# Late addition, accumulating transposes and predicated neighbour selection in a four-layer convolution kernel

## The chip, the cores and the metric

The kernel runs on one core of one Trainium2 chip. The metric is device time in microseconds (us). TensorE (PE), VectorE (DVE), ScalarE (ACT), GpSimd (POOL) and SyncE (SP) each run their own instruction stream and meet at semaphores. Everything is 32-bit float.

## The reference

x is 8 images of 64 channels, 96 x 96. Four layers in a row, each x + layer(groupnorm(x)):

```python
x = x + L0(gn(x))   # chunked linear attention (9 chunks of 1024 positions), group norm
x = x + L1(gn(x))   # offset conv, bilinear sampling at clipped offsets, 3x3 conv
x = x + L2(gn(x))   # 3x3 conv by FFT whose padded kernel makes it a sum over shifts
x = x + L3(gn(x))   # cosine similarities, offset-and-mask conv, deformable 3x3 conv
# L1, sampling at (cy, cx), both clipped to the image:
v_t = dy * (v_rt - v_lt) + v_lt
v_b = dy * (v_rb - v_lb) + v_lb
out = dx * (v_b - v_t) + v_t
# L3: four corners of each of 9 taps, gathered by index, weighted, masked, projected
val = (g00*(1-wy1)*(1-wx1) + g01*(1-wy1)*wx1 + g10*wy1*(1-wx1) + g11*wy1*wx1) * mask
out = einsum('bckhw,ock->bohw', val, weight)
```

## The kernel before

**Passes.** Two images fill the 128 partitions; there are four such pairs. `stage(p, prepare, sample, ahead)` is one pass. The first prepares pair 0 (layers 0 to 2, and of layer 3 the similarities, offsets, mask, and a table of pixels for gathering). The next three prepare pair p and sample pair p - 1, that is, carry out the gathers, weighting and projection of its layer 3. The fifth only samples.

**Sampling** is cut into 36 groups of 4 steps. For one step POOL issues 9 indirect DMAs (L643), one a tap, 128 positions each, into one of two buffers `gathered_corners`; it waits (L640) until the step before last is weighted. DVE weights them (`weigh`, L687), in one of three ways: with the sum over four corners left to PE (L703, `sum_on_pe`, into the single buffer `weighted_corners`, in the deform stage), with two sums on DVE (L705 to L710, elsewhere in a pass that prepares), or L716 to L722 (last pass). PE transposes (`turn`, L1367), with sum_on_pe by 20 accumulating matmuls against the identity (L1376), else by 5 transposes (L1379). ACT copies from PSUM (`turned`, L1132). After step 3 PE projects with 10 matmuls a half of a group (L1363), and DVE adds bias and residual (`finish`, L725, instruction L730). SP loads indices and weights (`load_meta`) and the residual (`load_res`) and stores the result (`store_out`). The tables `PLACES`, `CONV_PLACES`, `SUM_PLACES`, `COSINE_PLACES` and `OFFSET_PLACES` say at which place of the preparing work a step stands; `None` stands for `finish`. All engines follow the same tables, written out by hand.

**Preparing.** The stages are, in order: 9 chunks of attention (a group each), norms (one group, G_NORM), 12 deform tiles of 8 rows (a group each, G_TAPS), 12 pairs of convolution tiles (4 groups), the sums of layer 2 (4 groups), 24 tiles of cosines (2 groups), the offset stage (4 groups, G_OFFSETS).

**A deform tile.** PE makes the offsets (L1450, four banks of 9 matmuls). DVE reads and clips them to u and v (L872 to L875), makes the horizontal differences of the padded image (L879) and the maximum (L880), which PE turns (L1458) for a test whether any offset is 2 or more. Then for each of five rows ia = 0 to 4 the horizontal neighbours are combined and weighted with the row's hat (ACT), and summed. If sampling, this is done by four products a row (`product`, L891) with weights `cx` made on ACT, and four combinations (`combine`, L894). If not, ACT writes the left differences as defaults (`default_neighbours`, L1226), DVE replaces them by the right ones where v > 0 (`copy_predicated`, L941 and L942), and combines near and far with one product each (L947 to L952); `row_weight` is L928, `accumulate` L932.

**Offset stage.** For 12 pairs of row tiles PE makes offsets and mask from features and cosines (L1539, L1547), ACT adds the bias (L1326), PE turns them (L1556), ACT copies them out (L1330, `kept`). DVE, in four parts (h), does the steps of a group, copies the masks (L1078), computes coordinates (L1081 to L1098) and corner weights (L1102 to L1109) in one block, with ACT's sigmoid (L1335) between, then `finish`. SP feeds PE with cosines (`load_cosines`), two pairs ahead.

## Time and profile before

| | |
|---|---|
| median of 3 runs | 9312.17 us (9294.57 to 9316.33) |
| profiled execution | 9313.9 us, its span 9312.2 us |
| DVE busy | 6484.1 us, 70% of the span |
| POOL | 5527.0 us, 59% |
| PE (matmul) | 5348.9 us, 57% |
| ACT | 2144.6 us, 23% |
| mean granted PE clock | 0.754 of full speed |
| indirect DMAs issued by POOL | 5184, mean 1065 ns |

How to read it: busy shares are averages over the whole span. The first pass has no gathers (POOL idle for the first 15%), the last one nothing else (DVE at 40 to 50%). "issue" is time in which an engine waited for nothing that the profile shows. Times in the rows are in us from the start of the span.

### The profile page before, as it was taken

How to read it: one execution, taken by the hardware profiler on the slowest of the kernel's cores; microseconds unless marked ns; L12 is line 12 of the kernel's file. 1: busy time of each engine (PE TensorE's matmuls, PEld its weight loads, DVE VectorE, ACT ScalarE, POOL GpSimd, SP SyncE). 2: the span in 40 equal slices, each digit the busy share in tenths (PEclk: the TensorE clock that was granted, in tenths of full speed). 3: DMA queues.
4: the chain of work that ended last, by engine and by line, in shares of the span. 5: the costliest groups of instructions: out<-in, count | busy, mean ns of one | idle time of the engine just before them, and what ended most of it. 6: DMA issues, size and time to landing. Idle time of an engine off the chain costs nothing. (4 is left out here: it accounts for less than half of the span.)

```text
span 9312.2 us, 87129 instructions
## 1 busy us (share of the span) xinstructions
PE 5348.9 (57%) x26226; PEld 3344.0 (36%) x26226; DVE 6484.1 (70%) x7397; ACT 2144.6 (23%) x3640; POOL 5527.0 (59%) x5206
## 2 busy tenths in 40 slices
PE   4555766577766556577766556577766552222222
PEld 3333324355543234355543234355543231111111
DVE  5699547789985757789985757789985754444444
ACT  1344222223212312223212312223212310000000
POOL 0000007767667647767767647767767657777776
PEclk9877787788878777788887677788877775555555
DMA  2000133322233533332233533332233533333333
GB/s 73 20 0 0 43 93 107 101 94 79 76 103 105 161 114 105 100 95 79 75 103 107 158 117 105 101 96 79 75 103 105 159 101 113 112 113 113 113 112 104
DMA packets 443186, 887.37 MB, mean 95 GB/s; under 512 B 119072, under 2 KB 268918, under 8 KB 439924
## 3 DMA queue, kind: packets, MB, share of 16 engines
q0 software_dynamic: 248832, 679.81, 25.0%
q1 hardware_dynamic: 190708, 129.65, 4.7%
q10 hardware_dynamic: 3456, 75.50, 1.9%
q8 instruction: 105, 1.72, 0.1%
q14 instruction: 85, 0.70, 0.0%
HBM read 763.04 MB, written 121.53 MB: 95 GB/s over the span
## 5 line engine op out<-in xcount | busy, mean ns | idle before, releaser
L643 POOL DMA_INDIRECT gathered_corners<-gather_table,metas x5184 | 5518.7, 1065 | 3761.5 <-issue 2850.3
L1379 PE MATMUL ps<-ident,sampled 128*128 128x128 f32 (+1 forms) x2160 | 470.5, 369 | 2200.4 <-DVE sampled L722 1272.7
L1138 ACT COPY sampled_by_channel<-ps 128x512 f32<-128x512 f32 x576 | 336.7, 585 | 4158.0 <-PE ps L1379 3143.6
L1450 PE MATMUL ps<-region,woff 128*128 (+1 forms) x3456 | 1181.4, 498 | 23.6 <-ACT region L1123 23.6
L1379 PEld LDWEIGHTS ps<-ident,sampled 128*128 128x128 f32 (+1 forms) x2160 | 313.6, 178 | 2422.5 <-issue 2069.6
L705 DVE TENSOR_TENSOR gathered_corners<-gathered_corners,ps 128x2304 f32<-128x2304 f32 x288 | 735.5, 2554 | 534.3 <-DMA gathered_corners<-gather_table,metas 525.4
L1376 PE MATMUL ps<-ident,weighted_corners 128*128 128x128 f32 (+1 forms) x5760 | 850.0, 316 | 264.6 <-DVE weighted_corners L703 264.3
L1376 PEld LDWEIGHTS ps<-ident,weighted_corners 128*128 128x128 f32 (+1 forms) x5760 | 806.2, 218 | 346.0 <-issue 212.6
L1450 PEld LDWEIGHTS ps<-region,woff 128*128 128x128 f32 x3456 | 654.4, 192 | 499.1 <-issue 48.6
L1363 PE MATMUL ps<-sampled_by_channel,w 128*64 128x256 f32 x2880 | 709.8, 477 | 0.0
L891 DVE TENSOR_TENSOR work<-work 128x768 f32<-128x768 f32 x720 | 666.4, 954 | 5.0
L716 DVE TENSOR_TENSOR ps<-gathered_corners,ps 128x1152 f32<-128x1152 f32 x144 | 196.3, 1363 | 599.6 <-DMA gathered_corners<-gather_table,metas 598.4
L1363 PEld LDWEIGHTS ps<-sampled_by_channel,w 128*64 128x64 f32 x2880 | 410.6, 174 | 274.9 <-issue 166.3
L894 DVE TENSOR_TENSOR work<-work 128x768 f32<-128x768 f32 x540 | 498.6, 950 | 1.2
L730 DVE SCALAR_TENSOR_TENSOR ob<-ps,chan,res 128x256 f32<-128x256 f32 x144 | 69.7, 484 | 587.3 <-PE ps L1363 584.5
L707 DVE TENSOR_TENSOR gathered_corners<-gathered_corners 128x1152 f32<-128x1152 f32 x288 | 391.1, 1358 | 9.9
L703 DVE TENSOR_TENSOR weighted_corners<-gathered_corners,ps 128x2304 f32<-128x2304 f32 x144 | 367.9, 2555 | 15.1
L1486 PE MATMUL ps<-region,wconv 64*64 64x384 f32 x3456 | 337.0, 549 | 44.8 <-DVEq L983 41.7
L1458 PE MATMUL ps<-ident,small 128*1 128x128 f32 x96 | 28.1, 395 | 553.1 <-DVE small L880 553.1
L1539 PE MATMUL ps<-region,wcm 128*64 128x384 f32 x1728 | 296.5, 488 | 0.0
L1212 ACT ACTIVATE work<-work,taps 128x768 f32<-128x768 f32 x180 | 168.5, 936 | 318.3 <-DVE work L917 231.7
L710 DVE TENSOR_TENSOR sampled<-gathered_corners 128x576 f32<-128x576 f32 x288 | 218.4, 758 | 32.4 <-DVE gathered_corners L707 3.0
(230 smaller groups left out, 7991.4 us busy)
## 6 DMA issues: line engine op xcount, KB each, us to landing
gathered_corners<-gather_table,metas POOLq DMA_INDIRECT x5184
x_after_layer<-region ACTq DMA_DIRECT2D x8, 4608.0 KB, 12.4
gather_table<-tabst SPq DMA_DIRECT2D x192, 192.0 KB
region<-in_x_dram ACTq DMA_DIRECT2D x12, 1536.0 KB, 9.5
region<-x_after_layer ACTq DMA_DIRECT2D x4, 4608.0 KB, 16.0
res<-x_after_layer SPq DMA_DIRECT2D x144, 128.0 KB
out_dram<-ob SPq DMA_DIRECT2D x144, 128.0 KB
indices_and_weights<-region SPq DMA_DIRECT2D x16, 810.0 KB
```

Source lines behind the costliest of these rows:

```text
L643: pool.indirect_dma_start(out=G[:, s % NG, k, :], out_offset=None, in_=table, in_offset=bass.IndirectOffsetOnAxis(ap=idx[:, s * KK + k:s * ...
L703: ins = ch.after().tensor_tensor(W[:].rearrange("p q (k c) -> p q k c", c=C), Gq, w4, ALU.mult)
L705: ch.own(ch.after().tensor_tensor(Gs, Gs, w.unsqueeze(2).to_broadcast([128, 4 * KK, C]), ALU.mult))
L707: ch.own(ch.after().tensor_tensor(G2[:, :, 0:2 * C], G2[:, :, 0:2 * C], G2[:, :, 2 * C:4 * C], ALU.add))
L891: return ch.own(ch.at(earlier).tensor_tensor(rows(to), rows(cx[:, q]), steps_x[:, ia:ia + DROWS, q:q + HW], ALU.mult))
L894: return ch.own(ch.at(earlier).tensor_tensor(to, to, other, op))
L1138: nc.scalar.copy(VT[:, i, 0:4, 128 * t2:128 * t2 + 128], ps[:, 5, :].rearrange("p (k n) -> p k n", k=4))
L1363: mm = pe.matmul(ps[64 * i:64 * i + 64, 7, 0:GN], w3[:, k, :], VT[:, i, k, :], start=k == 0, stop=k == 4, tile_position=(0, 64 * i))
L1376: mm = pe.matmul(out_m, W[:, q, 128 * m:min(128 * m + 128, KK * C)], ident[:, :], start=q == 0, stop=q == 3)
L1379: mm = pe.transpose(out_m, V[:, s % 2, 128 * m:min(128 * m + 128, KK * C)], ident[:, :])
L1450: mm = pe.matmul(ps[:, b, 0:RN], woff[:, e, k, :], conv_rhs(pad2_1, 2, j * 16 + 4 * b, k // 3 - 1, k % 3 - 1), start=k == 0, stop=k == KK - 1)
L1486: mm = pe.matmul(ps[to, b + i, 0:RN], wconv[im, k, im], rhs[im], start=k == 0, stop=k == KK - 1, tile_position=(64 * i, 64 * h))
```

## The change

Four things are done together.

- In every pass the deform tiles use the predicated form; the form with four products is gone.
- `finish(g)` is taken from behind step 3 of group g to behind step 1 of group g + 1 (in the last pass too); `None` leaves the tables. SP loads metadata first, then stores the group before and loads the residual.
- The 20 matmuls of `turn` with sum_on_pe get `is_transpose=True`.
- In the offset stage ACT applies the sigmoid as it copies each pair out (array `masks`), DVE's block is cut into `coordinates` and `corner_weights`, which stand between the steps by the new table `META_PLACES`, and ACT's and PE's steps are spread over 13 places instead of 3 a part.

```diff
-          1: (((0, 0),), (), ((0, 1),), ((0, 2),), ((0, 3),), ((0, None),))}
+          1: (((0, 0),), (), ((0, 1),), ((0, 2),), ((0, 3),), ())}
-CONV_PLACES = ((0,), (1, 2), (3, None))
-SUM_PLACES = ((0,), (), (), (1,), (), (), (2,), (), (3,), (), (), (None,))
-COSINE_PLACES = ((), (0,), (), (), (1,), (), (), (2,), (), (3,), (), (None,))
-OFFSET_PLACES = ((0, 1), (2,), (3,))
+CONV_PLACES = ((0,), (1, 2), (3,))
+SUM_PLACES = ((0,), (), (), (1,), (), (), (2,), (), (3,), (), (), ())
+COSINE_PLACES = ((), (0,), (), (), (1,), (), (), (2,), (), (3,), (), ())
+OFFSET_PLACES = (((0, 0), (0, 1)), ((0, 2),), ((0, 3),), ((1, 0),), ((1, 1),), ((1, 2),), ((1, 3),),
+                 ((2, 0),), ((2, 1),), ((2, 2),), ((2, 3),), ((3, 0),), ((3, 1), (3, 2), (3, 3)))
+META_PLACES = {(1, 0): ((0, 0),), (1, 1): ((0, 1),), (1, 3): ((1, 0),), (2, 0): ((1, 1),), (2, 2): ((2, 0),), (2, 3): ((2, 1),),
+               (3, 1): ((3, 0),), (3, 2): ((3, 1),)}
...
-                def group(g, e, last=False):
-                    load_res(g)
+                def group(g, e, first=False, last=False):
                     if not last:
                         sp.wait_ge(weighted, g * STEPS + CREDIT)
                         load_meta(g + 1, 1 - e)
-                    store_out(g)
+                    if not first:
+                        store_out(g - 1)
+                    load_res(g)
...
+                for q in range(PAIRS):
+                    load_cosines(q, q % 2)
+                    if sample and q in (3, 7):
+                        g = G_OFFSETS + (q + 1) // 4
+                        sp.wait_ge(weighted, g * STEPS + CREDIT)
+                        load_meta(g + 1, (g + 1) % 2)
+                    if sample and q in (6, 10):
+                        g = G_OFFSETS + (q + 1) // 4
+                        store_out(g - 1)
+                        load_res(g)
+                    if q in (7, 10):
+                        store_meta(q // 3 - 2)
...
-                def steps_of(g, slot, steps, sum_on_pe=True):
+                def steps_of(g, slot, steps, sum_on_pe=True, first=False):
                     if sample:
                         for s in steps:
-                            if s is None:
-                                finish(g)
-                            else:
-                                weigh(g, slot, s, sum_on_pe)
+                            weigh(g, slot, s, sum_on_pe)
+                            if s == 1 and not first:
+                                finish(g - 1)
...
-                        if sample:
-                            def product(ia, q, to, earlier):
-                                if ia == 0:
-                                    v.wait_ge(parts_x, t * 4 + PART_ORDER.index(q) + 1)
-                                return ch.own(ch.at(earlier).tensor_tensor(rows(to), rows(cx[:, q]), steps_x[:, ia:ia + DROWS, q:q + HW], ALU.mult))
...
-                for h in range(PARTS):
-                    steps_of(h + G_OFFSETS, (h + G_OFFSETS) % 2, (2, 3) if h == 0 else (0, 1, 2, 3), False)
-                    v.wait_ge(om_tcp, h * (PAIRS // PARTS) + (PAIRS // PARTS + 2))
...
-                    ch.named(ch.after().tensor_copy(mk, sig[:, :, :, 18:27]), sig_in, h + 1)
...
+                for h in range(PARTS):
+                    for s in ((2, 3) if h == 0 else (0, 1, 2, 3)):
+                        steps_of(h + G_OFFSETS, (h + G_OFFSETS) % 2, (s,), False)
+                        for part, piece in META_PLACES.get((h, s), ()):
+                            (coordinates, corner_weights)[piece](part)
                     ch.restart()
+                if sample:
+                    finish(GROUPS - 1)
...
                 def kept(q, e):
                     act.wait_ge(om_tr, q + 3)
...
+                    for h in range(2):
+                        t0 = q * 6 + h * 3
+                        nc.scalar.activation(masks[:, t0:t0 + 3], turned_om[:, h, :, 0:54].rearrange("p a (i c) -> p a i c", i=2)[:, :, :, 18:27],
+                                             ACT.Sigmoid)
...
                                 mm = pe.matmul(out_m, W[:, q, 128 * m:min(128 * m + 128, KK * C)], ident[:, :],
-                                               start=q == 0, stop=q == 3)
+                                               start=q == 0, stop=q == 3, is_transpose=True)
```

## Rows read from the trace of the kernel before

**Rows 1.** Busy time by stretch: window, length, PE, PEld, DVE, ACT, POOL, clock, DMA share, GB/s

```profile
420.00:963.00 543.00, 288.83 (x828) 160.33 (x832) 503.02 (x548) 259.60 (x311) 0.00 (x0) 0.75 0.00 1
3505.00:3925.00 420.00, 281.35 (x1209) 187.54 (x1210) 322.90 (x320) 104.18 (x160) 323.42 (x318) 0.72 0.36 106
4017.00:4800.00 783.00, 589.75 (x2961) 441.50 (x2962) 734.86 (x741) 237.17 (x312) 551.78 (x428) 0.85 0.26 77
7680.00:9312.00 1632.00, 382.81 (x1440) 235.83 (x1440) 718.80 (x792) 106.52 (x288) 1217.89 (x1289) 0.57 0.38 111
```

**Rows 2.** Groups of DVE in 4017 to 4800: busy us, mean ns, idle before, releaser

```profile
L891 DVE TENSOR_TENSOR work<-work 128x768 f32<-128x768 f32 x240 | 222.2, 955 | 1.7
L703 DVE TENSOR_TENSOR weighted_corners<-gathered_corners,ps 128x2304 f32<-128x2304 f32 x48 | 122.6, 2555 | 5.0
L730 DVE SCALAR_TENSOR_TENSOR ob<-ps,chan,res 128x256 f32<-128x256 f32 x11 | 5.3, 484 | 17.2 <-PE ps L1363 17.2
```

**Rows 3.** Timeline of DVE, one sampled tile of the third pass: start, length

```profile
4283.62 1.75 DVE L880 TENSOR_REDUCE small<-work 128x1 f32<-128x1536 f32 x1
...
4349.20 1.75 DVE L880 TENSOR_REDUCE small<-work 128x1 f32<-128x1536 f32 x1
```

**Rows 4.** Timeline of DVE, one tile of the first pass

```profile
648.46 1.75 DVE L880 TENSOR_REDUCE small<-work 128x1 f32<-128x1536 f32 x1
...
670.98 1.06 DVE L941 COPY_PREDICATED work<-work 128x768 f32<-128x768 int32 x1
...
678.18 1.04 DVE L941 COPY_PREDICATED work<-work 128x768 f32<-128x768 int32 x1
...
693.96 1.75 DVE L880 TENSOR_REDUCE small<-work 128x1 f32<-128x1536 f32 x1
```

**Rows 5.** Group of POOL in 4017 to 4800

```profile
L643 POOL DMA_INDIRECT gathered_corners<-gather_table,metas x428 | 553.7, 1294 | 231.5 <-issue 123.1 <-DVE weighted_corners L703 108.4
```

**Rows 6.** Group of POOL in 7680 to 9312, the last pass

```profile
L643 POOL DMA_INDIRECT gathered_corners<-gather_table,metas x1289 | 1218.7, 945 | 392.7 <-issue 389.6 <-DVE sampled L722 3.0
```

**Rows 7.** Timeline of POOL in a sampled tile; in brackets the idle time before

```profile
4311.10 0.94 POOL L643 DMA_INDIRECT gathered_corners<-gather_table,metas  x1 [6.25 <-DVE weighted_corners L703]
4312.35 1.43 POOL L643 DMA_INDIRECT gathered_corners<-gather_table,metas  x1 [0.30 <-issue]
```

**Rows 8.** Offset banks alone (L1450), first pass: window, length, PE, PEld, clock

```profile
650.80:655.60 4.80, 4.80 (x8) 2.68 (x9) 0.50 0.00 0
655.60:676.80 21.20, 21.17 (x66) 11.94 (x64) 1.00 0.00 0
```

**Rows 9.** Timeline of PE: deform tile, offset stage, last pass

```profile
4322.78 4.75 PE L1376 MATMUL ps<-ident,weighted_corners 128*128 128x128 f32 x40
...
4338.12 3.67 PE L1363 MATMUL ps<-sampled_by_channel,w 128*64 128x256 f32 x20
...
5383.73 0.71 PE L1379 MATMUL ps<-ident,sampled 128*128 128x128 f32 x5
...
8501.10 1.33 PE L1379 MATMUL ps<-ident,sampled 128*128 128x128 f32 x5 [6.97 <-DVE sampled L722]
```

**Rows 10.** Waits before L730: us, times, longest; 3925 to 4017, 4800:5007, 5007:5210

```profile
DVE ob L730 <- PE ps L1363: 13.0, 2, 7.5
...
DVE ob L730 <- PE ps L1363: 25.7, 5, 6.2
...
DVE ob L730 <- PE ps L1363: 14.0, 2, 7.5
```

**Rows 11.** Timeline of DVE in the offset stage

```profile
5366.07 2.55 DVE L705 TENSOR_TENSOR gathered_corners<-gathered_corners,ps 128x2304 f32<-128x2304 f32 x1 [10.57 <-DMA gathered_corners<-gather_table,metas]
...
5393.70 0.33 DVE L1078 COPY region<-work 128x324 f32<-128x324 f32 x1 [22.82 <-ACT work L1330]
...
5428.00 2.56 DVE L705 TENSOR_TENSOR gathered_corners<-gathered_corners,ps 128x2304 f32<-128x2304 f32 x1 [9.25 <-DMA gathered_corners<-gather_table,metas]
...
5560.76 0.48 DVE L730 SCALAR_TENSOR_TENSOR ob<-ps,chan,res 128x256 f32<-128x256 f32 x1
```

**Rows 12.** Timeline of DVE in the last pass

```profile
8539.09 0.48 DVE L730 SCALAR_TENSOR_TENSOR ob<-ps,chan,res 128x256 f32<-128x256 f32 x1 [7.18 <-PE ps L1363]
```

More of the change, by code:

```diff
@@ L526, in _ @@
                     group(GROUPS - 2, 0)
-                    group(GROUPS - 1, 1, True)
+                    group(GROUPS - 1, 1, last=True)
+                    store_out(GROUPS - 1)
                     sp.wait_ge(out_stored, 16 * (GROUPS + 1))
@@ L823, in _ @@
                 ch.restart()
-                with v.Fori(0, NCHUNK - 1) as c:
-                    chunk(c, False)
-                chunk(NCHUNK - 1, True)
+                chunk(0, first=True)
+                with v.Fori(1, NCHUNK - 1) as c:
+                    chunk(c)
+                chunk(NCHUNK - 1, last=True)
                 group_norm(1, 18, EPS, affine=True)
@@ new lines, in _ @@
+                        ch.after()
+                        whole = weighted_row = None
+                        for ia in range(2 * R + 1):
+                            n, f = near_steps[ia % 2], far_steps[ia % 2]
+                            straight = pad2_1[:, bass.ds(y0 + ia, DROWS), R:R + HW]
+                            v.wait_ge(defaults, t * 5 + (ia + 1))
+                            v.nop().then_inc(defaults_seen, 1)
+                            f_chosen = ch.own(v.copy_predicated(rows(f), rows(right_side).bitcast(I32), steps_x[:, ia:ia + DROWS, R + 1:R + 1 + HW]))
+                            n_chosen = ch.own(v.copy_predicated(rows(n), rows(right_side).bitcast(I32), steps_x[:, ia:ia + DROWS, R:R + HW]))
+                            if ia > 0:
+                                weighted_row = row_weight(ia - 1, whole)
+                            if ia == 0:
+                                v.wait_ge(parts_x, t + 1)
+                            f_part = ch.own(ch.at(f_chosen).tensor_tensor(f, far_w, f, ALU.mult))
+                            if ia > 1:
+                                accumulate(ia - 1, weighted_row)
+                            n_part = ch.own(ch.at(n_chosen).tensor_tensor(n, near_w, n, ALU.mult))
+                            f_whole = ch.own(ch.at(f_part).tensor_tensor(rows(f), rows(f), straight, ALU.add))
+                            whole = ch.own(ch.at(f_whole).tensor_tensor(n, n, f, ALU.add))
+                            place(ia + 1)
@@ L957, in _ @@
+                        weighted_row = row_weight(2 * R, whole)
+                        accumulate(2 * R, weighted_row)
                         ch.after()
@@ L1229, in _ @@
+                        ch.after()
+                        ch.named(nc.scalar.activation(near_w, near_w, ACT.Identity, bias=taps[:, 5:6], scale=-1.0), parts_x, t + 1)
+                        default_neighbours(1)
+                        for ia in range(2 * R + 1):
+                            if ia >= 2:
+                                place(ia - 2)
+                                default_neighbours(ia)
+                            act.wait_ge(hat_used, t * 5 + (ia + 1))
                             ch.after()
-                            ch.own(nc.scalar.activation(right_side, v_, ACT.Relu))
+                            ch.own(nc.scalar.activation(hy[:, ia % 2], u_, ACT.Abs, bias=taps[:, ia:ia + 1]))
@@ L1566, in _ @@
                     if q > 0:
[L1567 removed]
+                        offset_steps(q)
+                offset_steps(PAIRS)
         setup()
```

254 lines of the change are left out of this document (90 added, 164 removed).

## The prediction

> **What bounds the kernel now.** The page was read first: DVE is busy 70% of the span, POOL 59%, PE 57%, and the chain that ended last covers only the last pass. An average over stages says little, so the table of stages came next [rows 1]. The kernel has four kinds of stretch. (a) The first pass only prepares. Its deform stage (420 to 963) has no gathers; DVE is busy 503 of 543 us. (b) Passes 2 to 4 prepare one pair of images and sample the one before; of the third pass the table has the chunks (3505 to 3925) and the deform stage (4017 to 4800). (c) The rest of such a pass is six shorter stages, among them the offset stage (5318 to 5562). (d) The last pass only samples.
>
> In the deform stage of a sampled pass DVE is busy 735 of 783 us, PE 590, POOL 552: DVE sets the pace. One tile takes 4349.20 - 4283.62 = 65.6 us [rows 3], twelve tiles are the stage, three passes have it: 36 tiles, 2360 us. In the chunks the other rule holds: 318 gathers are busy 323.4 us, and POOL spends 0.30 us between two of them, which is 323 + 95 = 419 of 420 us [rows 1, 6]. In the last pass it is 1219 + 390 = 1609 of 1632 us [rows 6]. Both are POOL's; nothing that DVE, PE or ACT save there can shorten them. So the stage where the change can earn is the deform stage, then the places where POOL and DVE wait for one another between stages.
>
> **Deform tiles, DVE.** The old tile has 20 products (L891), 20 combinations (L894), 5 row weights and 4 sums: 49 instructions of about 0.955 us [rows 2]. The new one has 10 predicated copies, 20 other steps, 5 row weights and 4 sums: 39. The first pass runs exactly that code, and its tile takes 693.96 - 648.46 = 45.5 us; a predicated copy is 1.04 to 1.06 us, one row of taps 678.18 - 670.98 = 7.2 us [rows 4]. What a sampled tile has on top: four weightings of 2.56 us [rows 2] = 10.2, a copy of the weights and the addition of the result (0.3 and 0.5 us), some 0.5 us of starts: 11.5. Sum 57.0. About 1 us of it is hidden, since in the first pass DVE waits here for the transposed maximum and for ACT, and the first weighting now lies over that. DVE alone: 56 us.
>
> The late addition takes `finish` from the tile's end to behind step 1 of the next group. The eleven waits for the projection in this stage, 17.2 us or 1.6 a tile [rows 2], go; they are within the difference of 65.6 to 56, not beside it. What is late next in their place is nothing: by step 1 the projection has had a whole tile's start. SP's `load_res` now stands behind `store_out` of the group before; it is asked for one tile later.
>
> **Deform tiles, POOL.** A tile needs 36 gathers. In this stage one is busy 1.294 us on average, in the last pass 0.945, both with 0.30 us between [rows 5, 6]; the timeline shows two kinds, 0.94 to 0.95 and 1.43 us, the long ones while DVE runs instructions with two inputs in SBUF [rows 7]. By the mean, (1.294 - 0.945) / (1.43 - 0.945) = 72% are long. At that share POOL needs 36 x 1.594 = 57.4 us a tile; now it waits for DVE besides (108 us in the stage, 6.25 us in the row shown [rows 5, 7]). After the change this slack is gone: POOL's 57.4 stands against DVE's 56. DVE has fewer two-input instructions in a tile, which shortens some gathers, but no row shows a gather beside a predicated copy. Bounds: if a copy leaves POOL free, 54 us, DVE sets 56; if it holds POOL like the others, 57.4, with up to 1 us for buffers that come free late. The row nearest is the two-input one, so I take 57.4. Saving 65.6 - 57.4 = 8.2 us a tile, times 36 = **295 us**; bounds 250 (58.6) to 345 (56.0).
>
> The Trainium skill (SBUF — State Buffer, Who interferes with whom) says that a VectorE instruction with two SBUF inputs contends only with GpSimd reads, and that descriptor writing was not seen to stall behind `tensor_tensor`. By that rule all gathers would take 1.25 us, 45 a tile, and the tile would be DVE's 56, 50 us less in all. The trace disagrees here already: 1.43 us beside these very instructions [rows 7]. I keep to the row.
>
> **Deform tiles, PE and ACT.** Under the change 40 matmul records of a step (4.75 us at full clock) become 20 of transpose mode. Five of those take 0.71 us in a row at full clock and 1.33 at the lower one [rows 9], so 20 take 2.8 and 5.3. The offset banks take 21.2 / 66 = 0.32 us a record at full clock and 4.8 / 8 = 0.60 at the lower [rows 8], 18 records a bank: 5.8 or 10.8. PE per tile at full clock: 4 x 5.8 + 4 x 2.8 + 3.7 (projection [rows 9]) + 0.6 = 38.7 us of 57. PE is off the path; what it must not do is hand a step's transposes over late, since the weighted corners have one buffer. From the end of weighting 0: step 0 takes 5.3 (low clock), banks 0 and 1 up to 5 us low, then full: done at about 20, step 1 at 23; DVE wants that buffer at 2 x 6.3 + 2.6 + 0.6 + 7.2 = 23. Tight, and the reason why the transposes belong to the change: with the old 4.8 us a step and more DVE would wait 2 us or more here. ACT goes from 18 to 26 activations of at most 0.95 us a tile, 25 us plus 3.4 of copies: covered by a 57 us tile; its order (old taps' place, then defaults) asks for step 0 long before DVE needs row 2. I cost ACT and PE at nothing; if step 1 came 2 us late in every tile, it would be 72 us.
>
> **Late addition elsewhere.** In chunks and in the last pass DVE stands before L730 for 4 to 7 us a group (7.18 in the row [rows 12]), but POOL is the bound: 0. At ends of stages DVE's wait is on the path: 13.0 us before the deform stage, 25.7 in five waits by the convolution, 14.0 in two by the 3x3 sums [rows 10]. The first pair I count whole; of the others only the last of a stage, 6 + 6 us, since before it DVE waits for gathers anyway. 25 us a pass, **75** in three; bounds 30 (only the first pair, partly) to 105.
>
> **Offset stage.** Now coordinates, corner weights and `finish` stand in one block of 14 us behind step 3, and POOL, two buffers ahead, stops; DVE then waits for it (9.25 us at 5428.00), and before that for the first offsets (22.82 us before L1078) [rows 11]. After the change each piece (about 5 and 8.5 us) lies between two steps, 11.25 us apart by POOL. From the last step of group 32 at 5366.07, twelve steps of 9 x 1.25 us remain: 135 us. One hold is left, since coordinates of part 0 still need the offsets at 5393.7: they end at 5399, step 1 of group 33 at 5403.5, and POOL loses 8 us. Last gathers land at 5509 to 5512, weighting and the last part's weights to 5519, then 7.2 us as in the last pass [rows 12]: 5527 against 5561 now. 34 us a pass, say **105** for three with the copy of the masks gone. The masks' sigmoids move to ACT's evictions (two short ones a pair of rows), which has idle time. What can take from it: SP's `load_cosines(8)` is queued behind the wait for all of group 33's steps, and PE's pair 8 behind that; V has two buffers, so up to 11 us are covered. Bounds 60 to 125. First pass: one copy and a wait less in four parts, 3 us.
>
> **Sum.** 295 + 75 + 105 + 3 = 478. The profiled run took 9313.9 us (its span 9312.2, the median of the runs 9312.2, so nothing to shift). 9314 - 478 = **8836 us**, 5.1% less.
>
> **Rivals.**
> (1) PE becomes the bound, and it is slower than before. Mechanism: PE's clock stays low. The trace: the granted clock of the stage is 0.85, so about 30% of it is at 1.2 GHz [rows 1]. All at 1.2 GHz a tile would cost PE 4 x 10.8 + 4 x 5.3 + 7.4 (the projection doubled) + 0.6 = 72.4, about 74 with the wait for the first step: 36 x 8.4 = 302 more, less 180: 9436 us. It decides once low clock covers more than 2 x (57 - 38.7) = 37 us of a tile; now it is 20. Against it: in the first pass the four banks alone, 26 us of 45.5, hold 0.75 [rows 1, 8]. The Trainium skill (TensorE: Matmul & The Clock Gate, Part 4: PE-mode transpose) has a rule for it, that transposes do not count as PE busy; then only the banks would raise the clock, as in that first pass, 0.75 or half of 57 us low: still under 37. Chance 0.04.
> (2) A predicated copy holds POOL longer than a two-input instruction, as three streams are read: a gather beside it at 1.9 instead of 1.43 us, ten or so a tile: 62 us. Saving 130 instead of 295: 9000. Nothing in the profile speaks on it. Chance 0.10.
> (3) The accumulating transposes are no cheaper than matmuls (the change does not do what it says): 3 us a tile, 110: 8945. The transposes of L1379 speak against it. Chance 0.05.
> (4) Late addition and offset stage bring nothing, since POOL or SP's queue takes it up: 9314 - 295 = 9019. For it: POOL's bound in the neighbouring stages. Chance 0.08.
> (5) More: POOL free beside the copies, every term at its upper bound: 9314 - 578 = 8736 and less. Chance 0.05.
>
> **How the numbers follow.** The forecast has the remaining 0.68. Its terms at their ends give 9314 - 340 = 8974 and 9314 - 578 = 8736. The range that holds 8 in 10 leaves out rival 1 and the farther part of 2, 4 and 5, some 0.18 in all: 8740 to 8990. Faster by over 0.3% (what a measurement of this kernel can tell from no change) 0.94, within it 0.02, slower 0.04 (rival 1).
>
> **What would show it.** In the changed profile a middle tile should be 56 to 58.5 us from one L880 to the next, with DVE over 90% busy and POOL's wait for DVE near zero; gathers of about 1.43 us beside COPY_PREDICATED (0.95 or 1.9 would be the ends). The transposes should be 20 records a step in under 3 us at full clock, the clock of the stage not under 0.75. No wait of L730 for PE outside a pass's end. In the offset stage 45 to 46 us a group after the first. The last pass should stay at 45.0 us a group. Waits of DVE for transposes in the tiles, or a POOL that works without a pause at 62 us a tile, would make it wrong.

## The result

The changed kernel takes 9151.99 us (median of 4 runs, 9143.02 to 9156.62), the kernel before 9310.42 us beside it: a ratio of 0.9831, 95% interval 0.9814 to 0.9848. It is 158 us faster; 478 were forecast, and 9152 lies outside the range of 8740 to 8990. What follows tells where the other 320 us went. The profiled run spans 9154.9 us.

The first lines of its page (busy time of each engine):

```profile
span 9154.9 us, 81120 instructions
## 1 busy us (share of the span) xinstructions
PE 4956.1 (54%) x23346; PEld 3000.0 (33%) x23346; DVE 6187.0 (68%) x7021; ACT 2312.3 (25%) x4008; POOL 5818.7 (64%) x5206
```

DVE and PE have less work, as meant. POOL issues the same 5184 gathers, yet it is busy 5818.7 us in place of 5527.0. The windows of the changed kernel that answer to [rows 1] (chunks, deform stage, last pass):

```profile
3440.00:3860.00 420.00, 263.79 (x1191) 178.68 (x1191) 319.20 (x313) 102.22 (x157) 324.35 (x315) 0.77 0.36 105
...
3960.00:4720.00 760.00, 482.19 (x1974) 333.70 (x1974) 620.52 (x607) 285.85 (x400) 631.43 (x423) 0.80 0.27 78
...
7520.00:9154.00 1634.00, 377.96 (x1440) 232.63 (x1440) 718.43 (x792) 106.52 (x288) 1219.69 (x1291) 0.57 0.38 111
```

In the deform stage DVE is busy 620.52 of 760 us (735 of 783 before), and POOL 631.43 for 423 gathers (551.78 for 428). Chunks and last pass hardly move. The groups of the deform stage say who waits for whom now (busy us, mean ns, idle before, releaser):

```profile
L654 POOL DMA_INDIRECT gathered_corners<-gather_table,metas x423 | 632.7, 1496 | 128.9 <-issue 128.9
...
L714 DVE TENSOR_TENSOR weighted_corners<-gathered_corners,ps 128x2304 f32<-128x2304 f32 x48 | 122.6, 2554 | 110.4 <-DMA gathered_corners<-gather_table,metas 107.8
L917 DVE COPY_PREDICATED work<-work 128x768 f32<-128x768 int32 x59 | 61.7, 1046 | 3.1 <-DVE small L897 3.1
```

The gather that took 1294 ns on average [rows 5] takes 1496. POOL has no idle time but its 0.3 us of issue; its waits for DVE (108.4 us [rows 5]) are gone, and DVE waits 107.8 us for gathers instead. The stage has changed its bound from DVE to POOL. The first gather of the stage's first group and that of the group behind the stage, 775.06 us apart:

```profile
3942.01 0.94 POOL L654 DMA_INDIRECT gathered_corners<-gather_table,metas  x1 [0.30 <-issue]
...
4717.07 0.94 POOL L654 DMA_INDIRECT gathered_corners<-gather_table,metas  x1 [0.30 <-issue]
```

That is 64.6 us a tile; by the same measure the kernel before has 786.7 us, 65.6 a tile. All "us a tile" below are this length over 12 in the third pass. Split in this way between first gathers of groups, the 157.3 us between the two spans are: 35 in the three deform stages (forecast 295), 79 in the offset stages up to the next pass (forecast 105), 37 in the other stages (53 less 16 that the chunks lose; forecast 75), 6.5 in the first pass (3), 0 in the last.

**What holds the gathers.** One tap row of the changed kernel, DVE and POOL by their timelines:

```profile
4267.13 1.05 DVE L917 COPY_PREDICATED work<-work 128x768 f32<-128x768 int32 x1
4268.06 1.04 DVE L918 COPY_PREDICATED work<-work 128x768 f32<-128x768 int32 x1
4268.98 0.97 DVE L904 TENSOR_TENSOR work<-work 128x768 f32<-128x768 f32 x1
4269.84 0.97 DVE L923 TENSOR_TENSOR work<-work 128x768 f32<-128x768 f32 x1
4270.71 0.97 DVE L908 TENSOR_TENSOR region<-region,work 128x768 f32 x1
4271.57 0.97 DVE L926 TENSOR_TENSOR work<-work 128x768 f32<-128x768 f32 x1
4272.44 0.97 DVE L927 TENSOR_TENSOR work<-work,region 128x768 f32<-128x768 f32 x1
4273.45 0.96 DVE L928 TENSOR_TENSOR work<-work 128x768 f32<-128x768 f32 x1
...
4268.00 0.97 POOL L654 DMA_INDIRECT gathered_corners<-gather_table,metas  x1 [0.30 <-issue]
4269.27 4.97 POOL L654 DMA_INDIRECT gathered_corners<-gather_table,metas  x1 [0.30 <-issue]
4274.55 0.94 POOL L654 DMA_INDIRECT gathered_corners<-gather_table,metas  x1 [0.31 <-issue]
```

A gather begins at 4269.27, 0.29 us into L904, the instruction behind the second copy. It passes the starts of L923, L908, L926 and L927 (0.87 us apart) and ends at 4274.24, 0.79 us after L928 starts. L928 reads what L927 in front of it writes, so it waits until L927 is through, and DVE runs empty for a moment. In the kernel before a gather beside such instructions ends behind the next start, at 1.43 us [rows 7]. Of the 1296 gathers in the three deform stages 154 take more than 2 us, up to 6.7; before there is none.

### The profile page after: what moved, and what is told of

Its sections match the earlier page's. It is cut to its first block and busy times, and to the rows that moved or that the text cites. A ratio compares the mean times of both kernels' runs of the same rounds, so it can differ in the third digit from the quotient of the medians.

```text
span 9154.9 us, 81120 instructions
## 1 busy us (share of the span) xinstructions
PE 4956.1 (54%) x23346; PEld 3000.0 (33%) x23346; DVE 6187.0 (68%) x7021; ACT 2312.3 (25%) x4008; POOL 5818.7 (64%) x5206
## 5 line engine op out<-in xcount | busy, mean ns | idle before, releaser
L654 POOL DMA_INDIRECT gathered_corners<-gather_table,metas x5184 | 5810.4, 1121 | 3312.1 <-issue 2867.2
L1348 PE MATMUL ps<-ident,weighted_corners 128*128 128x128 f32 (+1 forms) x2880 | 536.3, 368 | 521.5 <-DVE weighted_corners L714 521.4
L1348 PEld LDWEIGHTS ps<-ident,weighted_corners 128*128 128x128 f32 (+1 forms) x2880 | 482.0, 188 | 602.6 <-issue 438.3
L1196 ACT ACTIVATE work<-work 128x768 f32<-128x768 f32 x240 | 201.6, 840 | 831.3 <-DVE region L908 721.2
L709 DVE COPY ps<-metas 128x144 f32 (+1 forms) x144 | 44.7, 310 | 506.9 <-DMA gathered_corners<-gather_table,metas 474.6
L917 DVE COPY_PREDICATED work<-work 128x768 f32<-128x768 int32 x240 | 250.9, 1045 | 13.4 <-DVE small L897 13.4
L918 DVE COPY_PREDICATED work<-work 128x768 f32<-128x768 int32 x240 | 249.4, 1039 | 0.0
```

What stands on the lines that cost most here:

```text
L654: pool.indirect_dma_start(out=G[:, s % NG, k, :], out_offset=None, in_=table, in_offset=bass.IndirectOffsetOnAxis(ap=idx[:, s * KK + k:s * ...
L917: f_chosen = ch.own(v.copy_predicated(rows(f), rows(right_side).bitcast(I32), steps_x[:, ia:ia + DROWS, R + 1:R + 1 + HW]))
L1348: mm = pe.matmul(out_m, W[:, q, 128 * m:min(128 * m + 128, KK * C)], ident[:, :], start=q == 0, stop=q == 3, is_transpose=True)
```

## Experiments

Theory A, formed on these rows: behind a predicated copy a gather cannot begin its work until DVE runs empty, that is, until an instruction is through before the next one starts. Its rivals change with what the runs leave of it. Unless another is named, an edit is made to the changed kernel. Experiments 2, 7, 8, 10, 11, 14 and 15 are single runs; their readings rest on tiles and gathers of the trace more than on the time.

**1. DVE waits for the second copy** before it starts the next instruction.

```diff
                             n_chosen = ch.own(v.copy_predicated(rows(n), ...))
+                            v.wait_ge(*n_chosen)
```

> The changed kernel, with one wait more in each row of a deform tile: DVE waits for its second predicated copy to be done before it goes on. Theory A: after a predicated copy DVE keeps POOL from the port through the instructions that follow it, until DVE has once run empty (in the changed kernel only at the row's last addition, L928, hence gathers of 4 to 5 us). Then the boundaries behind the new wait let POOL in again, the long gathers fall to about 1.4 to 1.7 us, their mean in the deform stage from 1.50 to 1.30 us or less, a tile from 64.8 to 57 to 59 us, and the kernel takes 9152 - 36 x 6.5 = 8920 us. Theory B: the copies are innocent; POOL gets the port only where an instruction waits for the one directly in front of it. Then the new wait is one more such place a row, but the run from there to L928 is as long as before: gathers of 4 us stay, the tile is 62 to 65 us, the kernel 9060 to 9150 us.

Measured: 8908.62 us (8904.82 to 8917.31), ratio 0.9572 (0.9556 to 0.9588). Five gathers over 2 us are left, the longest 2.7. The groups of its deform stage, the window, and one tap row by the timeline:

```profile
L654 POOL DMA_INDIRECT gathered_corners<-gather_table,metas x427 | 548.6, 1285 | 132.8 <-issue 128.6 <-DVE weighted_corners L714 4.1
...
L714 DVE TENSOR_TENSOR weighted_corners<-gathered_corners,ps 128x2304 f32<-128x2304 f32 x48 | 122.6, 2554 | 10.9 <-DMA gathered_corners<-gather_table,metas 6.2
```

```profile
3890.00:4570.00 680.00, 457.57 (x1995) 311.10 (x1996) 636.23 (x613) 287.71 (x402) 547.55 (x427) 0.83 0.31 89
```

```profile
4267.34 1.06 DVE L918 COPY_PREDICATED work<-work 128x768 f32<-128x768 int32 x1
4268.44 0.96 DVE L904 TENSOR_TENSOR work<-work 128x768 f32<-128x768 f32 x1
4269.31 0.95 DVE L924 TENSOR_TENSOR work<-work 128x768 f32<-128x768 f32 x1
...
4268.55 1.67 POOL L654 DMA_INDIRECT gathered_corners<-gather_table,metas  x1 [0.30 <-issue]
```

The gather of 4268.55 begins in L904 too, 0.11 us into it, and now ends 0.91 us after the next start. DVE pays 1.10 instead of 0.92 us from copy to product; tiles fall from 64.6 to 57.3 us. One wait is worth 0.9831 - 0.9572 = 2.6%, some 240 us, and gives the tile of the forecast (57.4). Theory B, which expected gathers of 4 us to stay, falls.

**2. No predicated copy at all**: both become a maximum of two SBUF inputs (the choice of neighbours of layer 1 is left out).

```diff
-f_chosen = ch.own(v.copy_predicated(rows(f), rows(right_side).bitcast(I32), steps_x[...]))
-n_chosen = ch.own(v.copy_predicated(rows(n), rows(right_side).bitcast(I32), steps_x[...]))
+f_chosen = ch.own(v.tensor_tensor(rows(f), rows(f), steps_x[...], ALU.max))
+n_chosen = ch.own(v.tensor_tensor(rows(n), rows(n), steps_x[...], ALU.max))
```

> The changed kernel with both predicated copies of a row replaced by a maximum of the same two operands (so the neighbour is not chosen by the sign and layer 1 is another function; the order of instructions, their waits and their operands otherwise are the same). Theory A (the state that a predicated copy leaves): no gather over 2 us is left in the deform stage, the mean is 1.30 us or less, tiles 56 to 58 us, the kernel 8880 to 8900 us. Theory B (only an instruction that waits for the one in front lets POOL in): gathers of 4 to 5 us stay, tiles 64 us, the kernel about 9120 to 9150 us.

Measured: 8859.0 us (21 under the range of theory A), tiles 56.4 us, gathers 1.257 us on average, one over 2 us. Number, place and waits of DVE's instructions are those of the changed kernel; the kind differs, and with it each of the two takes 0.1 us less. The length of the gathers is the copies' doing.

**3. Every product and sum waits for the one in front of it** (`ch.at(...)` becomes `ch.after()` in L904 to L928).

> The changed kernel; in the rows of a deform tile each of the products and sums waits for the instruction directly in front of it. DVE pays about 0.12 us for each of 29: a tile of 56 becomes 59.5 us for DVE alone. Both theories expect short gathers here (mean 1.1 to 1.3 us), since DVE runs empty behind every instruction: tiles 59 to 61 us, 9152 - 36 x 5 = 8970 us. If gathers stay at 1.5 us in the mean, both theories fall and it is the time that DVE's two-input instructions hold the port at all.

Measured: 9045.79 us, ratio 0.9722 (0.9706 to 0.9739). Tiles of 59.8 us with gathers of 1.25 us: DVE runs empty at every start, POOL is as free as it can be, and DVE pays for it. The time is 75 us over the expectation, of which the first pass takes 48 (its first gather comes at 1433 instead of 1385 us): I had not counted that its tiles run the same code.

**4. The old form with four products back** in the sampling passes, the other three parts of the change kept.

```diff
+                        if sample:
+                            (product and combine, as in the kernel before; on ACT its weights cx)
+                        else:
```

> The changed kernel with the four-product form back in the sampled passes, so that late addition, accumulating transposes and the new offset stage act alone. By the theory that the predicated copies brought almost nothing because POOL became the bound, the tile is 65.6 less the wait for the projection, 1.5: 64.1 us, gathers at 1.29 us again, and the whole is 9140 to 9165 us, within 0.3% of the changed kernel. Rival: the copies brought the larger part of the 158 us, and this kernel takes 9220 us or more.

Measured: 9128.85 us (9122.64 to 9129.65), ratio 0.9808 (0.9791 to 0.9824); tiles 63.6 us. The three other parts alone bring about 180 us. The predicated copies, the part with the largest term in the forecast, bring nothing as written: with them the kernel is 23 us slower by the medians (the two intervals overlap), and its three deform stages are 40 us longer in the traces; with the wait they bring 220.

**5. Plain summing matmuls** instead of transposes (`is_transpose=True` dropped), on the kernel of experiment 1.

> The kernel with the wait behind the copies (e1_drain), but with the 20 summing matmuls of a step as plain matmuls again. By the prediction's own step (its rival 3), a step's sum then takes 4.8 us and more instead of 2.8, the buffer of weighted corners comes free about 2 us late for DVE in the middle steps: 2 to 4 us a tile, 36 tiles, so 8909 + 110 = 9020 us (8980 to 9050). Rival: PE has enough room and DVE waits for gathers anyway at these places; then it is within 15 us of e1_drain.

Measured: 8926.01 us, ratio 0.9585 (0.9569 to 0.9601), tiles 57.7 us: the transposes are worth 17 us in all by the medians, and the intervals of 1 and 5 overlap. So the price of rival 3 for a buffer that comes free late, 110 us, is refuted, and the rival (within 15 us) is nearly met. The transposes of one step, first in the changed kernel, then here, both at full clock; below them the deform stage here:

```profile
4303.51 2.35 PE L1348 MATMUL ps<-ident,weighted_corners 128*128 128x128 f32 x20
```

```profile
4270.91 4.75 PE L1349 MATMUL ps<-ident,weighted_corners 128*128 128x128 f32 x40
```

```profile
3905.00:4595.00 690.00, 570.27 (x3021) 424.48 (x3023) 636.40 (x612) 283.79 (x395) 545.77 (x430) 0.90 0.30 91
```

The transposes of a step take half the time, but PE is not the bound. The granted clock is also lower with them, 0.83 against 0.90. The Trainium skill (TensorE: Matmul & The Clock Gate, Part 4: PE-mode transpose) says that transposes do not count as busy in the way matmuls do; the two clocks agree with it, though the transposes are fewer too, and these runs do not part the two.

**6. The addition of a group directly behind its step 3**, on the kernel of experiment 1.

```diff
-                            if s == 1 and not first:
-                                finish(g - 1)
+                            if s == STEPS - 1:
+                                finish(g)
...
```

> The kernel with the wait behind the copies (e1_drain), but with the addition of a group's result back behind step 3 of its own group (SP's order as in the changed kernel). By the theory that it matters where DVE sets the pace: 1.5 us in each of 36 deform tiles, and some 16 us a pass between the stages, less up to 5 us a pass in the chunks, which have grown from 427 to 432 us with the late addition: 8909 + 54 + 48 - 15 = 8996 us. Rival: the tiles are now as much POOL's as DVE's, so only the stage ends count: 8909 + 48 - 15 = 8942 us.

Measured: 9251.19 us, ratio 0.9935 (0.9918 to 0.9951); both numbers expected are missed. DVE stands before the addition in every tile of the deform stage, 79.3 us in 12:

```profile
L654 POOL DMA_INDIRECT gathered_corners<-gather_table,metas x427 | 530.0, 1241 | 222.0 <-issue 122.8 <-DVE weighted_corners L714 99.2
...
L741 DVE SCALAR_TENSOR_TENSOR ob<-ps,chan,res 128x256 f32<-128x256 f32 x12 | 5.8, 484 | 79.3 <-PE ps L1332 79.3
```

This is not the place of the kernel before, which had other work between step 3 and the addition; so it was not the undoing that I took it for. Experiment 9 is.

**7 and 8. One predicated copy more a row** in the kernel of experiment 4 (old form); in 8 the next product waits for it. Both copy into a buffer that is then overwritten. In both DVE also waits for the last use of that buffer in front of the copy, so it runs empty there, once a row.

```diff
+v.wait_ge(*free3)
+v.nop().then_inc(defaults_seen, 1)
+extra = ch.own(v.copy_predicated(rows(b3), rows(v_).bitcast(I32), steps_x[:, ia:ia + DROWS, R:R + HW]))
-product(ia, 3, b2, free2)
+product(ia, 3, b2, free2)     # in 8: extra instead of free2
-p0 = product(ia, 0, b3, free3)
+p0 = product(ia, 0, b3, extra)
```

> The kernel with four products (e4_oldtaps), with one predicated copy more in front of each row of a deform tile, into a buffer that the next product but one overwrites, so the result is the same; DVE does not run empty between this copy and the row's last addition. Theory A (a copy leaves the port held until DVE runs empty) expects gathers of 7 to 9 us, one in each row, and tiles of 80 us and more instead of 63.5: above 9700 us. Theory that a copy only holds the port during its own microsecond: 5 x 1.1 us a tile, 69 us, 9330 us.

> The same extra copy in front of each row, but the next product waits for it, so DVE runs empty once behind it. Theory A expects gathers as in e4_oldtaps again (none over 2.5 us, mean about 1.3 us) and tiles of 69 us, the copy's own time and the wait: 9129 + 36 x 5.8 = 9340 us. If the copy itself were the cause and not what follows it, this kernel would be as slow as e7_onecopy.

Measured: 9341.72 us without the wait (tiles 69.6 us), 9334.59 with it (68.9 us; no gather over 2 us). The second is as expected, the first is not: theory A in its simple form wanted over 9700. Long gathers are there, but only 33 in three stages, about one a tile:

```profile
4241.65 1.06 DVE L921 COPY_PREDICATED work<-work 128x768 f32<-128x768 int32 x1
...
4241.99 9.32 POOL L654 DMA_INDIRECT gathered_corners<-gather_table,metas  x1 [0.30 <-issue]
...
4250.65 1.06 DVE L921 COPY_PREDICATED work<-work 128x768 f32<-128x768 int32 x1 [0.15 <-DVE region L934]
```

This one began while the copy ran and sat 9.32 us, past nine instructions, until DVE had run empty at 4250.65. Most others of that kernel were served at the next start. So the copy does not close the way to every gather behind it, and since POOL has slack here (DVE sets the tile at 69), the few long ones cost little: the three deform stages are 25 us longer than in 8.

**9. The addition at the old places**, on the kernel of experiment 1 (tile's end, end of a chunk, of three convolution tiles, of a block of offsets, of a group of the last pass).

> The kernel with the wait behind the copies (8909 us), but DVE's addition of a group back at the places of the kernel before (tile's end, end of a chunk, of three convolution tiles, of a block of offsets, of a group of the last pass). Theory A (the forecast's terms): 1.6 us a tile in 36 tiles = 58, transitions 16 to 19 us a pass as the two traces show = 52, less 4 us a pass that late addition cost in the chunks = 12: 9007 us. Rival B: in the deform stage POOL is as long as DVE (57.2 us a tile in both cases), so only the transitions count: 8950 us.

Measured: 8957.33 us (8948.86 to 8960.99), ratio 0.9623 (0.9607 to 0.9639). Rival B holds: late addition is worth 49 us here, none of it in the deform stage (57.3 us a tile both ways; DVE waits 1.4 us for the projection in the whole stage), and less than none in the chunks (425.9 against 431.8 us). By first gathers, the traces of the two (31.6 us apart, less than the medians) put 38 us on the other stages between chunks and offsets and 22 on the offset stages; the chunks take back 20, and some 8 us the other way lie in the deform stages and in the first and last pass.

**10 and 11. The wait at another place**: behind the row weight L904 that follows the copies, or between the two copies.

```diff
                                 weighted_row = row_weight(ia - 1, whole)
+                            v.wait_ge(*(weighted_row if ia > 0 else n_chosen))
```

```diff
                             f_chosen = ch.own(v.copy_predicated(rows(f), ...))
+                            v.wait_ge(*f_chosen)
                             n_chosen = ch.own(v.copy_predicated(rows(n), ...))
```

> DVE runs empty one instruction later: it does not wait behind the second copy, but behind the row weight that follows it (in row 0, where there is none, behind the copy). Theory A (any place where DVE runs empty frees POOL; a gather is held from the first copy to there): the hold of a row grows by 0.96 us in four rows of a tile, some 3.5 us a tile of POOL's time beyond DVE's slack of a microsecond: tiles 60 to 61 us, 9025 to 9045 us, longest gathers near 3.7 us. Rival C (only a wait on the copy itself frees it): four of five rows hold as in the changed kernel, tiles 63 to 64 us, 9110 to 9150 us.

> DVE waits between the two copies (for the first) and not behind the second. Theory A (each predicated copy starts a hold that ends when DVE runs empty): the second copy starts it again, tiles 63.5 to 64.6 us, 9110 to 9150 us, gathers up to 5 us. Rival D (the hold comes from two copies that run into one another): tiles 57.5 us, 8920 us, gathers under 2.8 us.

Measured: 10 takes 8927.21 us, tiles 58.0 us, longest gather 3.4 us; 11 takes 9027.51 us, tiles 60.8 us, longest 5.15. The first refutes rival C: the wait need not be for a copy, DVE need only run empty, and one instruction later costs 19 us in the three deform stages. It misses theory A's numbers too (60 to 61 us, 9025 to 9045): of the 129 gathers that begin in L904 none takes over 1.53 us, since the next start, behind which it would be served anyway, is the one that waits. The second is between both expectations. Its timelines say why: of the 144 gathers of the three stages that began in L904 directly behind the second copy, all 0.08 to 0.19 us into it, 50 sat until DVE ran empty and 94 were served at the next start. Without a wait between the copies (the changed kernel, 0.24 to 0.31 us into L904) it is 120 against 19. A gather asked behind a copy is passed over often, not always; once passed over, it waits for DVE to run empty.

**12. The addition on time in the chunks alone**, on the kernel of experiment 1.

```diff
-                    steps_of(c, slot, (1,), False, first)
+                    steps_of(c, slot, (1,), False, True)
...
+                    if sample and not last:
+                        finish(c)
```

> The kernel with the wait behind the copies, but in the chunks 0 to 7 DVE adds a group at the chunk's end, as the kernel before does. Theory A: the chunks go from 432.5 back to 428 us a pass, three passes: 8909 - 13 = 8896 us. Rival B (the 4 us come from something else, such as SP's order of loads): 8909 us.

Measured: 8894.26 us (8893.18 to 8896.09), ratio 0.9554 (0.9538 to 0.9570); the chunks take 426.7 us in place of 431.8. The time is as expected; its interval overlaps that of experiment 1, but the chunks are shorter in all three passes. Late addition loses in the chunks by DVE's order, not by SP's.

**13. The wait in sampling passes alone**, on the kernel of 12 (`if sample:` before it).

> The kernel with the wait behind the copies and the on-time addition in the chunks (8894 us), the wait now in the sampling passes alone. Theory A: the first pass has no gathers, so its 60 waits only cost; the first gather came at 1400.5 with them and 1385.1 without: 8894 - 15 = 8879 us. Rival B (the 15 us are scatter between runs, as first gathers between 1385 and 1392 in runs without waits suggest for a part): 8888 us or more.

Measured: 8881.03 us (8875.92 to 8887.37), ratio 0.9539 (0.9523 to 0.9555). 13 us less by the medians, as theory A expects, but the intervals of 12 and 13 overlap, and of the 18.9 us between the two traces only 5.4 lie in the first pass; the rest is in later stages that the edit does not touch. Over all traces the first gather comes at 1397 to 1401 us with these waits (experiments 1, 5, 6, 9, 12) and at 1385 to 1392 without: some 10 us for 60 waits that nobody needs, 0.17 us each. By its median this is the fastest version that computes the same function: 4.6% under the kernel before, and 2.9% of it beyond the change as written.

**14 and 15. One copy of the pair alone**, without any wait: the first stays (14) or the second (15), the other is a maximum.

> The changed kernel without any wait; of the two copies of a row the first stays, the second is a maximum of two SBUF inputs (the choice of near neighbours of layer 1 is left out). Theory A2 (only a gather that asks while DVE runs the instruction directly behind a copy can be missed, and then waits until DVE runs empty): a gather served at the boundary between the two asks again 1.25 us later, which is behind the maximum, so next to none is missed: tiles 56.4 to 57.5 us, 8860 to 8900 us, longest gathers near 2 us. Rival C (any copy since DVE last ran empty is enough): tiles 63 to 64.6, 9100 to 9150 us. Rival D (it takes two copies in a row): 57 us and 8880 here.

> The changed kernel without any wait; the first copy of a row is a maximum (the choice of far neighbours of layer 1 is left out), the second stays. Theory A2: the gather served at the boundary between the two asks again 1.25 us later, 0.3 us into the instruction directly behind the copy, and is missed as in the changed kernel: tiles 61 to 64.6 us, 9030 to 9150 us, gathers of 4 to 5 us. Rival C: the same. Rival D (two copies in a row): tiles 57 us, 8880 us.

Measured: 14 takes 8906.45 us (tiles 56.9 us, 57.5 and 58.0 in the other two passes, 10 gathers over 2 us), 15 takes 9083.99 us (tiles 62.0 us, 118 of them). Both fit theory A2 but for 6 us over its range and gathers of up to 7 us in 14, and they refute its rivals: any copy since DVE last ran empty would have made 14 slow, two in a row are not needed in 15. One row of 14, then one of 15:

```profile
4239.96 1.04 DVE L917 COPY_PREDICATED work<-work 128x768 f32<-128x768 int32 x1
4240.90 0.94 DVE L918 TENSOR_TENSOR work<-work 128x768 f32<-128x768 f32 x1
4241.76 0.94 DVE L904 TENSOR_TENSOR work<-work 128x768 f32<-128x768 f32 x1
...
4242.09 1.44 POOL L654 DMA_INDIRECT gathered_corners<-gather_table,metas  x1 [0.30 <-issue]
```

```profile
4277.12 1.05 DVE L918 COPY_PREDICATED work<-work 128x768 f32<-128x768 int32 x1
4278.06 0.94 DVE L904 TENSOR_TENSOR work<-work 128x768 f32<-128x768 f32 x1
...
4278.33 4.97 POOL L654 DMA_INDIRECT gathered_corners<-gather_table,metas  x1 [0.30 <-issue]
```

In 14 the gather begins one instruction further from the copy and takes 1.44 us; in 15 it begins in the instruction behind the copy and takes 4.97. What decides first is what DVE runs when the gather begins, and that is a matter of rhythm: a gather served at one start is through and begins again 1.2 us after it, the starts are 0.87 to 0.93 us apart, so it falls into the instruction next to the one that started then. Where the start was that of the second step of a row, as in most rows, the next is L904: directly behind the last copy in the changed kernel and in 15, one further in 14. Counted over whole traces, this is only half of it:

| kernel | begins directly behind the last copy: gathers, held | begins in a copy: gathers, held |
|---|---|---|
| changed | 175, 151 | 180, 5 |
| 15 (second copy alone) | 174, 120 | 25, 0 |
| 11 (wait between the copies) | 180, 53 | 180, 0 |
| 7 (extra copy, old form) | 43, 19 | 137, 13 |
| 14 (first copy alone) | 3, 1 | 179, 8 |

(Held means that it takes more than 2 us.) Experiment 7 has few long gathers in part because few begin at the bad place, 43 against 175, and in part because fewer of these are held, 19 of 43; the second is not explained. A gather that begins while a copy itself runs is mostly served at the next start; where it is not, it is held longest, 6.99 us in the one of 14 in the third pass, 9.32 in that of 7. So theory A2 holds for most gathers, not for all.

## Why the prediction was wrong, point by point

**Deform tiles, DVE: right, but it does not decide.** DVE alone was put at 56 us; without its waits for gathers the changed kernel's DVE needs 64.6 - 107.8 / 12 = 55.6. The first pass kept its tile (DVE busy 503.59 us from 418 to 960; 503.02 in [rows 1]).

**Deform tiles, POOL: the step that failed.** "If it holds POOL like the others, 57.4" took a predicated copy to hold a gather as a two-input instruction does, since "the row nearest is the two-input one". The bounds, 250 to 345 us, rested on the same. The term of 295 us came in at 35, and even that is not the copies': against experiment 4 they lengthen the three deform stages by 40 us, and the other parts shorten them by 75. In its place: a gather that begins directly behind a copy is held past four starts (4.97 us) instead of being served at the next (1.43), POOL's mean goes to 1.496 us, and the tile to 64.6. Take the hold away and the term is right: three stages of experiment 1 save 301 us against 295. Rival 2 named the mechanism (a copy holds POOL longer, chance 0.10) but sized it at 1.9 us for a gather beside the copy itself; the gathers behind it, at 3.2 to 5 us, it did not see, and its 9000 was too low as well; its reason, that three streams are read, no run tests. The sign to look for stood in the text: "a POOL that works without a pause" at 62 us a tile. It came, at 64.6. What the Trainium skill (SBUF — State Buffer, Who interferes with whom) reports, that descriptor writing did not stall behind `tensor_tensor`, does not carry over to these gathers: in experiment 2 no copy is left and they still average 1.257 us against 0.945 in the last pass [rows 6]. But the prediction took the section to mean that gathers stay free. It also says that two SBUF inputs contend with GpSimd's reads, and a gather reads its indices from `metas`, which lies in SBUF; so the section may be right here, and no run parts the two readings. Another sentence of it holds: an instruction with at most one SBUF input, outside the two-port modes, leaves GpSimd alone, as the gathers of 0.94 to 0.95 us beside the 2.55 us weightings show.

**PE and ACT: cover right, reason wrong.** 20 records in under 3 us at full clock were forecast and 2.35 measured; the stage's clock is 0.80, over the 0.75 asked. But "with the old 4.8 us a step and more DVE would wait 2 us or more here" failed: in the kernel with the wait, plain matmuls cost 17 us (0.4 us a tile). The records are cheaper, as forecast, and it makes next to no difference. Rival 1 (PE's clock) did not show, in either form.

**Late addition: half.** 75 forecast, 37 found in the traces. Experiment 9 has 49 by the medians, but 22 of its 31.6 us in the traces lie in the offset stages, which the forecast had in another term; the stages of this term give 38 less 20 for the chunks. The waits of L730 at the ends of stages [rows 10] went, some 18 us a pass against 25. What the sum had at nothing, the chunks, costs 5 us a pass, since "POOL is the bound: 0" forgot that a moved instruction can also delay. Why late addition is slower there was not traced further than to DVE's order. The 1.6 us a tile that the waits of [rows 2] stood for "within the difference" were indeed no separate gain in the new form.

**Offset stage: three quarters.** 79 of 105 us, 26 a pass against 34; some 7 a pass of it are the late addition's, by experiment 9. The groups behind the first take 59.7, 48.2 and 46.4 us in the third pass (76.1, 51.0 and 49.7 before) instead of 45 to 46. One hold of POOL of 8 us was forecast; three are there, and a wait that the text did not name, DVE before its last sum of a step for PE's transposes:

```profile
5302.77 0.76 DVE L721 TENSOR_TENSOR sampled<-gathered_corners 128x576 f32<-128x576 f32 x1 [6.61 <-PE ps L1351]
5312.20 0.69 DVE L1058 TENSOR_TENSOR region<-work,by 128x162 f32<-128x162 f32 x2 [8.68 <-ACT work L1305]
...
5304.34 0.95 POOL L654 DMA_INDIRECT gathered_corners<-gather_table,metas  x1 [3.61 <-DVE sampled L721]
5322.85 0.99 POOL L654 DMA_INDIRECT gathered_corners<-gather_table,metas  x1 [7.52 <-DVE sampled L721]
5337.63 0.94 POOL L654 DMA_INDIRECT gathered_corners<-gather_table,metas  x1 [3.44 <-DVE sampled L721]
```

3.61 + 7.52 + 3.44 = 14.6 us instead of 8. PE's steps are spread over its pairs, so a step's transposes stand behind the next pair's offsets (PE had waited 18.51 us for cosines at 5281.09); I had checked SP's and ACT's order there and not this one. That it is the cause of the whole 8 us a pass was not tried by a run.

**First pass within scatter, last pass right.** 3 us forecast, 6.5 found; first gathers scatter as much between runs (1385 to 1392 us where there is no wait), so this neither shows nor refutes the 3 us; the last pass takes 1641.7 us from its first gather in both kernels.

## What to carry to other kernels

Where GpSimd writes descriptors beside VectorE, a new kind of VectorE instruction can have a price on GpSimd of its own; when no row shows it, the nearest kind is no bound, and the range must reach to where it holds the other engine through the whole chain behind it. Where GpSimd is near the bound, try a wait for the last predicated copy directly behind it (some 0.2 us): it was worth 240 us here, more than the rest of the change. And measure a part's gain with the others kept: three of the four parts alone were at least as fast as all four.

## What the runs showed of the hardware

- A gather of 128 positions takes 0.945 us alone, and as much beside a weighting with one input in PSUM; 1.43 beside a run of two-input instructions in SBUF (served at the next start); 3.24, 4.10 or 4.97 when it begins directly behind a `COPY_PREDICATED` and is passed over, and 9.32 where DVE had nine instructions more before it ran empty. The Trainium skill (SBUF — State Buffer, Who interferes with whom) says of VectorE's two-port modes that the one who issues first has the shared ports for the whole instruction. Whether a predicated copy is such a case no run shows; these rows show a hold over several instructions.
- Whether it is passed over is not certain: of the gathers that begin in L904 behind the copy 120 of 139 in the changed kernel, 50 of 144 with a wait between the copies, with no difference in their offsets within a kernel. Of those that begin in a copy, 5 of 180. What decides in the single case stays open, and so does what in the copy does it: the operation, its mask or its three operands.
- A wait on the instruction just issued costs DVE 0.18 us from start to start (1.10 against 0.92), and 0.17 us by the first gathers (experiment 13).
- 20 accumulating 128x128 transposes of 32-bit values take 2.35 us at full clock, where 40 matmul records took 4.75; the stage's granted clock fell from 0.90 to 0.83 with them.
